# Two attention layers on one core: the first layer's products with the values in two sets, and the queries' piece moved between the key pieces

## The chip, the cores and the metric

The kernel runs on one core of a Trainium2 chip. The metric is the device time of one execution in microseconds. Three executions of the kernel before gave 2612.48 to 2613.71 us, median 2613.1 us.

## What is computed

The batch B is 32, with 112 queries of 320 channels each (20 heads of 16) and a context of 375 tokens of 512 channels, of which the first 77 are "text". Two cross-attention layers follow each other on the same context:

```python
# layer 0: text = ctx[:, :77], ip = ctx[:, 77:] (298 tokens); separate key and value weights for both
q = heads(x @ Wq.T)
out = softmax(q k_text / 4) v_text + softmax(q k_ip / 4) v_ip
x = out @ Wo.T + bo + x
# layer 1: text = the first 371 tokens, ip = the last 4
probs = softmax(q k_text / 4);  text_out = probs v_text
qsem = l2norm(probs text_ctx);  sem = qsem . l2norm(ip_ctx)
probs_ip = softmax(q k_ip / 4 + 0.5 sem) * spatial_mask
x = (text_out + probs_ip v_ip) @ W_out + b_out + x
```

## The kernel before

**One order of stages.** `stage_order` writes down one list of stages for all batches; each engine walks the list and issues its own part of each stage, in that order, with semaphores between the engines. A stage that waits on one engine holds up everything that stands behind it on the same engine. `share` and `in_bank` note for each user of a buffer which signal frees it. PSUM has a three-bank score buffer `ST`, one buffer `PN` of two banks called `PV` and `NS`, and three single banks `R`, handed out in a ring of three to all other products.

**One turn of the loop**, for batch b, has four parts: `groups0(b)`, layer 0 of batch b in five groups of four heads; `groups1(b - 1)`, layer 1 of the batch before; and the row maxima of both layers for what comes next. Among them stand the "pieces" of `ahead(b)`: products for batch n = b + 1 that depend on nothing near. `among0(g)` puts one piece behind the scores of each group of layer 0. Those pieces are, in their order: `keys(n, 0, 0)`, `keys(n, 0, 1)`, `keys(n, None, 0)`, `keys(n, 1, 0)`, then one piece that holds `text_keys(n)` and `queries(n, 0)`, then `keys(n, 1, 1)`; text values follow. `text_keys(n)` makes a third of the text keys of four later batches at once, in the 21 batches in which n is below 28 and no multiple of four. Where n leaves a remainder of three (n = 3, 7, ..., 27) that third holds rows of both layers.

**A group of layer 0** is twelve score matmuls (L690, L693) into `ST`, an exponential on ScalarE (L1126) into one of two buffers `p32`, and 16 matmuls with the values (L707, L710), in which four heads run side by side in strips of 32 columns, each with 17 columns of weights. An f32 matmul has two records, so a group has 32. In `groups0` the product of group g - 1 stands behind the scores and the piece of group g. It is copied by ScalarE to `pvt` (L1024, stage `pv0`), turned by TensorE with an identity (L721, L723, stage `pvT`) and divided and summed by VectorE. `PV_PARTS` says which groups one `pvT` takes: before, groups 0 and 1, then 2 and 3, then 4. The last `pvT` of a batch stands behind the scores of the next layer's first group.

**A key piece** is twelve matmuls (L583 to L587; text keys are eight records of L574 and L575) into a bank R. ScalarE copies the result as bf16 to `kst` (L1024, `kst<-R`), VectorE takes the remainder, a second bf16 part is made by ScalarE for even pieces (`kst<-rem`) and by VectorE for odd ones, and GpSimd makes the third (L1189). Then SyncE writes the three parts to `k_split` in DRAM (L1344; text keys L1340: four DMAs, or eight for the third with rows of both layers, behind which the next text tile `tx` is loaded, L1280). `kst` has two buffers, taken in turn by all key pieces in the order of the list, so the copy of a key piece waits until the writes of the piece two before have landed:

```python
w.wait_ge(k_mm, j + 1)
if j >= 2:
    for signal, value in kw_after[j - 2]:
        w.wait_ge(signal, value)
```

The queries go the same way to `q_split` (L1361, three DMAs). All DMAs are issued by SyncE in the order of the list, among them the `Qs<-ms` writes of the row maxima (L1379), the `xT` load and the reads of keys and queries for the score products (L1354, L1369).

**Layer 1** uses `p32` as well, plus `pr` for rounded probabilities and the two buffers `w2` for weighted ones; `w2` also receives the raw context of a coming batch for a while.

## Time and profile before

| | |
|---|---|
| median of three executions | 2613.1 us |
| the profiled execution's own time | 2613.9 us |
| its span, first to last instruction | 2612.1 us |
| granted TensorE clock, mean | 0.98 |
| TensorE matmuls busy | 2475.8 us (95%) |
| VectorE, ScalarE, GpSimd busy | 63%, 47%, 29% |
| DMA, share of 16 engines | 61.2% |

The busy share of TensorE counts a matmul from its start to its modelled end, and such spans overlap; a matmul takes longer than the distance to the next one. So distances between starts tell more than the busy time. Times in the rows are microseconds from the start of the span.

### The profile page before, as it was taken

What the parts mean: (1) busy time and instruction counts of PE and PEld (TensorE: products, weight loads), DVE (VectorE), ACT (ScalarE), POOL (GpSimd) and SP (SyncE); (2) the same over time, 40 slices, a digit from 0 to 9 for tenths busy, and PEclk for the clock granted to TensorE, in tenths of its full rate; (3) what the DMA queues carried; (4) which work ended last, traced back from release to release, by engine and by line L of the source; (5) the groups of instructions that cost most, each with busy time, mean ns of one, the idle gap of its engine ahead of it and who ended that gap; (6) DMA issues with size and microseconds to landing.
All of it is one profiled execution on the core that took longest, in us unless ns stands there. A gap on an engine that the chain in (4) does not pass through costs nothing.

```text
span 2612.1 us, 64042 instructions
## 1 busy us (share of the span) xinstructions
PE 2475.8 (95%) x26280; PEld 2128.5 (81%) x26280; DVE 1637.9 (63%) x3210; ACT 1232.6 (47%) x2305; POOL 767.3 (29%) x999
## 2 busy tenths in 40 slices
PE   6689999999999999999999999999999999999996
PEld 5578888888888888888888888888888888888874
DVE  2246765666765666776666676566676556677655
ACT  2334445544445544445544445544444544444543
POOL 2123323323323323323322332322322322333222
PEclk7799999999999999999999999999999999999997
DMA  7455777556677555677565777655677655567620
GB/s 181 104 97 87 104 103 93 83 92 92 95 103 91 96 89 86 95 100 107 83 90 86 93 110 101 85 88 86 99 96 104 89 86 89 87 94 101 89 38 7
DMA packets 493225, 241.46 MB, mean 92 GB/s; under 512 B 259627, under 2 KB 492923, under 8 KB 492924
## 3 DMA queue, kind: packets, MB, share of 16 engines
q1 hardware_dynamic: 492934, 237.37, 61.2%
q8 instruction: 208, 3.41, 0.6%
q14 instruction: 83, 0.68, 0.1%
HBM read 171.35 MB, written 64.59 MB: 90 GB/s over the span
## 4 chain that ended last, share of the span: by engine, by line
PE 76%; DVE 17%; issue 2%; SPq 2%; DMA 2%; ACT 1%; POOL 0%; DVEq 0%; ACTq 0%; POOLq 0%
PE ST L690 7%; DVE w L827 6%; PE PN L707 5%; PE R L734 5%; PE R L632 4%; PE R L645 4%; PE R L646 4%; DVE m L911 4%; PE R L583 4%; PE R L584 4%; PE PN L752 3%; PE R L648 3%; PE R L791 3%; PE R L586 3%; DVE w L824 3%; PE ST L672 2%
## 5 line engine op out<-in xcount | busy, mean ns | idle before, releaser
L1126 ACT ACTIVATE p<-ST 128x1344 f32<-128x1344 f32 x320 | 413.6, 1293 | 114.6 <-PE ST L693 110.1
L1256 POOL TENSOR_TENSOR w<-w 128x448 f32<-128x448 f32 (+1 forms) x256 | 330.8, 1292 | 426.3 <-DVE w L824 408.2
L827 DVE SCALAR_TENSOR_TENSOR w<-p,pr 128x1344 f32<-128x1344 f32 x160 | 296.7, 1854 | 174.9 <-ACT pr L1141 161.7
L824 DVE TENSOR_TENSOR rem<-R,kst 128x298 f32<-128x298 f32 (+2 forms) x184 | 91.4, 497 | 455.1 <-ACT kst L1024 455.1
L734 PE MATMUL R<-pr,Gh 128*128 128x448 f32 (+1 forms) x960 | 367.6, 383 | 0.0
L824 DVE TENSOR_TENSOR w<-R,w 128x448 f32<-128x448 f32 (+1 forms) x480 | 281.6, 620 | 71.5 <-PE R L739 61.1
L645 PE MATMUL R<-wvh,ch 128*128 128x320 f32 (+3 forms) x896 | 302.8, 338 | 16.3 <-ACT V0t L1024 12.6
L1189 POOL TENSOR_TENSOR kst<-rem,kst 128x298 bf16<-128x298 f32 (+2 forms) x184 | 151.2, 822 | 483.3 <-ACT kst L1024 262.0
L646 PE MATMUL R<-wvh,cl 128*128 128x320 f32 (+3 forms) x896 | 279.7, 312 | 0.0
L690 PE MATMUL ST<-Qs,Ks 100*128 100x112 bf16 (+1 forms) x3520 | 229.6, 214 | 14.7 <-DMA Qs<-ms 7.6
L690 PEld LDWEIGHTS ST<-Qs,Ks 100*128 100x128 bf16 (+1 forms) x3520 | 184.5, 98 | 67.5 <-issue 35.0
L583 PE MATMUL R<-ch,wkh 128*128 128x298 f32 (+1 forms) x640 | 218.3, 341 | 11.5 <-DVE wkl L824 11.5
L1024 ACT ACTIVATE pvt<-PN 128x112 f32<-128x112 f32 (+1 forms) x320 | 98.1, 306 | 252.7 <-PE PN L756 194.0
L648 PE MATMUL R<-wvl,ch 128*128 128x320 f32 (+3 forms) x672 | 209.7, 312 | 0.0
L1141 ACT ACTIVATE pr<-ST 128x1344 fp32r<-128x1344 f32 x160 | 205.2, 1282 | 0.0
L584 PE MATMUL R<-cl,wkh 128*128 128x298 f32 (+1 forms) x640 | 203.2, 318 | 0.0
L734 PEld LDWEIGHTS R<-pr,Gh 128*128 128x128 f32 (+1 forms) x960 | 176.7, 184 | 22.8 <-issue 6.2
L645 PEld LDWEIGHTS R<-wvh,ch 128*128 128x128 f32 (+3 forms) x896 | 163.3, 182 | 22.0 <-ACT V0t L1024 13.0
L737 PE MATMUL R<-pr,Gl 128*115 128x448 f32 (+1 forms) x480 | 177.1, 369 | 0.0
L739 PE MATMUL R<-pr,Gl 128*128 128x448 f32 (+1 forms) x480 | 176.0, 367 | 0.0
L915 DVE TENSOR_REDUCE m<-ST 112x3 f32<-112x1113 f32 x128 | 168.0, 1312 | 9.0 <-PE ST L674 9.0
L1024 ACT ACTIVATE V<-R 128x320 f32<-128x320 f32 (+2 forms) x160 | 67.6, 437 | 219.0 <-PE R L649 219.0
(185 smaller groups left out, 5834.2 us busy)
## 6 DMA issues: line engine op xcount, KB each, us to landing
Ks<-k_split SPq DMA_DIRECT2D x384, 140.6 KB, 6.1
Ks<-k_split SPq DMA_DIRECT2D x384, 93.8 KB, 8.3
Qs<-q_split SPq DMA_DIRECT2D x384, 70.0 KB, 8.2
w<-in_ctxT SPq DMA_DIRECT2D x31, 750.0 KB, 6.0
k_split<-kst SPq DMA_DIRECT2D x64, 281.2 KB, 3.3
k_split<-kst SPq DMA_DIRECT2D x64, 223.5 KB
q_split<-qst SPq DMA_DIRECT2D x128, 84.0 KB, 2.2
k_split<-kst SPq DMA_DIRECT2D x64, 111.8 KB, 2.5
```

The costliest lines, as they stand in the source:

```text
L583: e.matmul(r[:, 0:t1 - t0], wh[:, k, c0:c0 + 128], h[:, k, t0:t1], start=k == 0, stop=False)
L584: e.matmul(r[:, 0:t1 - t0], wh[:, k, c0:c0 + 128], lo[:, k, t0:t1], start=False, stop=False)
L645: e.matmul(r[0:n, 0:C], h[:, k, :], wh[:, k, :], start=k == 0, stop=False)
L646: e.matmul(r[0:n, 0:C], lo[:, k, :], wh[:, k, :], start=False, stop=False)
L648: e.matmul(r[0:n, 0:C], h[:, k, :], wl[:, k, :], start=False, stop=False)
L690: e.matmul(ST[:, u, S * h:S * h + S], Ks[l][0:m, GH * g + h, 128 * u:128 * u + 128], Qs[l][0:m, GH * g + h, :], start=True, stop=True)
L734: e.matmul(r[0:nj, 0:QW], Gh[0:ROWS[u], q:q + nj], x[0:ROWS[u], QW * u:QW * u + QW], start=u == 0, stop=False)
L824: return e.tensor_tensor(to, x, y, op)
L827: return e.scalar_tensor_tensor(out=to, in0=x, scalar=s, in1=y, op0=op0, op1=op1)
L1126: e.activation(p32[i][:].rearrange("p (u q) -> p u q", u=3), st, ACT.Exp).then_inc(p_whole, 1)
L1141: e.activation(pr[n % 2][:].rearrange("p (u q) -> p u q", u=3), ST[:, :, 0:QW], ACT.Exp).then_inc(p_round, 1)
L1256: e.tensor_tensor(first, first, w2[n % 2][0:ROWS[j], QW * j:QW * j + QW], ALU.add).then_inc(ns_added, 1)
```

## The change

The five products with the values of layer 0 are no longer one behind each group of scores. They come in two sets: groups 0, 1 and 2 in one run behind the scores and the piece of group 3, and groups 3 and 4 in one run behind the piece of the sixth slot. Groups 0, 1, 3 and 4 write two halves of `PV`, group 2 writes `NS`. The probabilities of five groups lie in `p32[0]`, `p32[1]`, `w2[0]`, `w2[1]` and `p32[0]` again. ScalarE copies two groups of `PV` in one instruction, and `NS` in another one. The first two `pvT` stand in the fifth and sixth slot; the parts are groups 0 and 1, then 2, then 3 and 4. The piece with text keys and queries moves from the fifth place to the second, before `keys(n, 0, 1)`. The bookkeeping of who frees what is rewritten to match.

```diff
--- before.py
+++ after.py
@@ -12,7 +12,8 @@
 QW = GH * S
 FV0, FV1 = D + 1, D + 1 + NIP
 ROWS = [128, 128, 115]
-PV_PARTS = [((0, 1), (2, 3), (4,)), ((0, 1, 2, 3), (4,))]
+PV_PARTS = [((0, 1), (2,), (3, 4)), ((0, 1, 2, 3), (4,))]
+PV_SETS = ((0, 1, 2), (3, 4))
 EPS2 = 1e-24
 QPART = [0, 1, 2, 0, 1, 0]
 KPART = [0, 0, 0, 1, 1, 2]
@@ -107,10 +108,10 @@
         todo = ((n, 0, 0), (b, 1, 0), (b, None, 0), (b, 1, 1), (b, None, 1), (b, 1, 2), (b, None, 2), (n, 0, 1), (n, 0, 2))
         tail = values([x for x in todo if x[0] < B])
         if n < B:
-            for l, m in ((0, 0), (0, 1), (None, 0), (1, 0)):
+            yield keys(n, 0, 0)
+            yield text_keys(n), queries(n, 0)
+            for l, m in ((0, 1), (None, 0), (1, 0), (1, 1)):
                 yield keys(n, l, m)
-            yield text_keys(n), queries(n, 0)
-            yield keys(n, 1, 1)
             yield text_values(n)
         yield from tail
 
@@ -142,16 +143,19 @@
         return n
 
     def groups0(b, between):
-        prev = None
+        first = uses[0]
         for g in range(NG + 1):
-            n = scores(b, 0, g) if g < NG else None
+            if g < NG:
+                scores(b, 0, g)
             between(g)
+            if g > 3:
+                turn(b, 0, g - 4)
             if g in (3, 5):
-                turn(b, 0, g // 2 - 1)
-            if g:
-                o.add("pv0", b, g - 1, prev)
-                o.share("PV", 1, ("pv", prev), "pv_read", prev + 1)
-            prev = n
+                which = g // 2 - 1
+                o.add("pv0", b, which, first)
+                o.share("PV", 1, ("pv0", b, which), "pv_read", first + (2, 5)[which])
+                if which == 0:
+                    o.share("NS", 1, ("pv0", b, which), "pv_read", first + 3)
 
     def turn(b, l, part):
         o.add("pvT", b, l, part)
@@ -545,6 +549,14 @@
 
         def rows(name):
             return a[name].rearrange("(k e) c -> e k c", e=128)
+
+        def p0_place(g):
+
+            return (p32[0][:], p32[1][:], w2[0], w2[1], p32[0][:])[g]
+
+        def pv0_place(g):
+
+            return ((PV, 0), (PV, 2 * S), (NS, 0), (PV, 0), (PV, 2 * S))[g]
 
         def v_place(l, t):
 
@@ -693,23 +705,27 @@
                     e.matmul(ST[:, 2, S * GH - S:S * GH], Ks[l][0:m, h, 256:384], Qs[l][0:m, h, :], start=True,
                              stop=True).then_inc(s_mm, 1)
                 elif kind == "pv0":
-                    b, g, n = key
-                    p = p32[n % 2]
+                    b, which, first = key
                     w.wait_ge(v_copied, at("v", b, 0, 2))
-                    w.wait_ge(p_whole, n + 1)
-                    free(w, "PV", ("pv", n))
-                    for u in range(-1, 3):
-                        k = TEXT0 if u < 0 else 119 if u == 2 else 128
-                        for h in range(GH):
-                            hh, q0 = GH * g + h, QW * max(u, 0) + S * h
-                            v, c = (V0t[0:k, hh, :], 0) if u < 0 else (V0[0:k, u, hh, :], S)
-                            if u < 2 or h < GH - 1:
-                                e.matmul(PV[32 * h:32 * h + FV0, c:c + S], v, p[0:k, q0:q0 + S], start=u < 0, stop=u == 2,
-                                         skip_group_check=True)
-                    h = GH - 1
-                    e.matmul(PV[32 * h:32 * h + FV0, S:2 * S], V0[0:119, 2, GH * g + h, :],
-                             p[0:119, 2 * QW + S * h:2 * QW + S * h + S], start=False, stop=True,
-                             skip_group_check=True).then_inc(pv_mm, 1)
+                    for g in PV_SETS[which]:
+                        p, to, c = p0_place(g), *pv0_place(g)
+                        w.wait_ge(p_whole, first + g + 1)
+                        if g in (0, 3):
+                            free(w, "PV", ("pv0", b, which))
+                        elif g == 2:
+                            free(w, "NS", ("pv0", b, which))
+                        for u in range(-1, 3):
+                            k = TEXT0 if u < 0 else 119 if u == 2 else 128
+                            for h in range(GH):
+                                hh, q0 = GH * g + h, QW * max(u, 0) + S * h
+                                v, c0 = (V0t[0:k, hh, :], c) if u < 0 else (V0[0:k, u, hh, :], c + S)
+                                if u < 2 or h < GH - 1:
+                                    e.matmul(to[32 * h:32 * h + FV0, c0:c0 + S], v, p[0:k, q0:q0 + S], start=u < 0,
+                                             stop=u == 2, skip_group_check=True)
+                        h = GH - 1
+                        e.matmul(to[32 * h:32 * h + FV0, c + S:c + 2 * S], V0[0:119, 2, GH * g + h, :],
+                                 p[0:119, 2 * QW + S * h:2 * QW + S * h + S], start=False, stop=True,
+                                 skip_group_check=True).then_inc(pv_mm, 1)
                 elif kind == "pvT":
                     b, l, part = key
                     r = R[slot["R", ("pvT",) + key]]
@@ -940,7 +956,7 @@
                     if i > 1:
                         w.wait_ge(pvT_read, i - 1)
                     if l == 0:
-                        c0 = 128 * part
+                        c0 = GH * D * PV_PARTS[0][part][0]
                         if 3 * b + part:
                             w.wait_ge(o_added, 3 * b + part)
                         if b:
@@ -1116,22 +1132,41 @@
                     copy(ms[0:n, 0, :], r[0:n, 0:S], -1.0).then_inc(m_hi, 1)
                 elif kind == "scores":
                     b, l, g, n = key
-                    i = n % 2
                     st = ST[:, :, 0:QW]
                     w.wait_ge(s_mm, n + 1)
-                    if n >= 2:
-                        w.wait_ge(pv_mm, n - 1)
-                        if l_of[n - 2][0] == 1:
-                            w.wait_ge(w_made, l_of[n - 2][1])
-                    e.activation(p32[i][:].rearrange("p (u q) -> p u q", u=3), st, ACT.Exp).then_inc(p_whole, 1)
-                elif kind in ("pv0", "pv1"):
+                    if l == 0:
+                        to = p0_place(g)
+                        w.wait_ge(pv_mm, n - 3 if g == 4 else n - g)
+                        if b > 1:
+                            w.wait_ge(w_made, NG * (b - 1))
+                        if g in (2, 3):
+                            w.wait_ge(c_low, 4 * min(B, b + 2))
+                            if b > 1:
+                                w.wait_ge(ns_mm, NG * (b - 1))
+                    else:
+                        to = p32[n % 2][:]
+                        w.wait_ge(pv_mm, n - min(g, 1))
+                        if g > 1:
+                            w.wait_ge(w_made, NG * b + g - 1)
+                    e.activation(to.rearrange("p (u q) -> p u q", u=3), st, ACT.Exp).then_inc(p_whole, 1)
+                elif kind == "pv0":
+                    b, which, first = key
+                    if b:
+                        w.wait_ge(pvT, at("pvT", b - 1, 0, 2 * which))
+                    w.wait_ge(pv_mm, first + (2, 5)[which])
+                    copy(pvt[0][:, 3 * which:3 * which + 2, :],
+                         PV[:, 0:4 * S].rearrange("p (g q) -> p g q", g=2)).then_inc(pv_read, 2)
+                    if which == 0:
+                        if b:
+                            w.wait_ge(pvT, at("pvT", b - 1, 0, 1))
+                        w.wait_ge(pv_mm, first + 3)
+                        copy(pvt[0][:, 2, :], NS[:, 0:2 * S]).then_inc(pv_read, 1)
+                elif kind == "pv1":
                     b, g, n = key
-                    l = int(kind == "pv1")
-                    part = [g in groups for groups in PV_PARTS[l]].index(True)
                     w.wait_ge(pv_mm, n + 1)
                     if b:
-                        w.wait_ge(pvT, at("pvT", b - 1, l, part))
-                    copy(pvt[l][:, g, :], PV[:, 0:(2 - l) * S]).then_inc(pv_read, 1)
+                        w.wait_ge(pvT, at("pvT", b - 1, 1, g // 4))
+                    copy(pvt[1][:, g, :], PV[:, 0:S]).then_inc(pv_read, 1)
                 elif kind == "p_round":
                     n, = key
                     k = at("p_round", n)
...
```

## Rows read from the trace of the kernel before

**Rows 1.** Page: busy time by engine; one kind of DMA, median us to landing.

```profile
PE 2475.8 (95%) x26280; PEld 2128.5 (81%) x26280; DVE 1637.9 (63%) x3210; ACT 1232.6 (47%) x2305; POOL 767.3 (29%) x999
...
k_split<-kst SPq DMA_DIRECT2D x64, 281.2 KB, 3.3
```

**Rows 2.** Timeline of TensorE, `groups0` of batch 16: start, duration, line, out<-in, count.

```profile
1332.77 0.72 PE L690 MATMUL ST<-Qs,Ks 102*128 102x112 bf16 x11
...
1335.02 0.30 PE L587 MATMUL R<-ch,wkl 128*128 128x298 f32 x1
1335.16 0.72 PE L690 MATMUL ST<-Qs,Ks 102*128 102x112 bf16 x11
...
1337.36 0.30 PE L587 MATMUL R<-ch,wkl 128*128 128x298 f32 x1
...
1338.48 0.71 PE L690 MATMUL ST<-Qs,Ks 102*128 102x112 bf16 x11
...
1344.82 0.27 PE L723 MATMUL R<-ident_sb,pvt 128*112 128x128 f32 x1
...
1345.91 0.71 PE L690 MATMUL ST<-Qs,Ks 102*128 102x112 bf16 x11
...
1346.52 1.78 PE L574 MATMUL R<-tx,wkt 128*128 128x308 f32 x6
...
1348.65 1.95 PE L632 MATMUL R<-xT,wq 128*128 128x128 f32 x16
...
1353.81 0.49 PE L721 MATMUL R<-ident_sb,pvt 128*112 128x128 f32 x3
...
1355.23 0.71 PE L690 MATMUL ST<-Qs,Ks 100*128 100x112 bf16 x11
```

**Rows 3.** Timeline of TensorE, a product of layer 1 with another behind it.

```profile
1306.07 0.67 PE L752 MATMUL PN<-p,V 128*21 128x112 f32 x19
...
1306.66 0.95 PE L769 MATMUL PN<-w,sel_sb 128*5 128x112 f32 x32
```

**Rows 4.** Timeline of ScalarE, batch 16: the second exponential and the last `pvt` copy.

```profile
1336.67 1.27 ACT L1126 ACTIVATE p<-ST 128x1344 f32<-128x1344 f32 x1
...
1355.37 0.36 ACT L1024 ACTIVATE pvt<-PN 128x224 f32<-128x224 f32 x1 [0.88 <-PE PN L710]
```

**Rows 5.** Timeline of SyncE, batch 16: start of the issue, its length.

```profile
1338.78 2.26 SPq L1379 DMA_DIRECT2D Qs<-ms  x3
...
1351.23 1.97 SPq L1340 DMA_DIRECT2D k_split<-kst  x4
```

**Rows 6.** Timeline of SyncE, batch 14: text keys of both layers.

```profile
1196.83 6.00 SPq L1340 DMA_DIRECT2D k_split<-kst  x8
...
1203.52 1.68 SPq L1361 DMA_DIRECT2D q_split<-qst  x3
```

**Rows 7.** Timeline of SyncE near the start, where text keys stand among others.

```profile
28.41 3.06 SPq L1340 DMA_DIRECT2D k_split<-kst  x4
...
36.92 5.28 SPq L1340 DMA_DIRECT2D k_split<-kst  x8
...
42.89 1.23 SPq L1344 DMA_DIRECT2D k_split<-kst  x2
```

**Rows 8.** Timeline of ScalarE, same stretch; brackets: idle ahead, and its releaser.

```profile
34.61 0.43 ACT L1024 ACTIVATE kst<-R 128x308 bf16<-128x308 f32 x1 [6.78 <-DMA k_split<-kst]
...
44.63 0.48 ACT L1024 ACTIVATE kst<-R 128x371 bf16<-128x371 f32 x1 [6.63 <-DMA k_split<-kst]
45.72 0.51 ACT L1024 ACTIVATE kst<-rem 128x371 bf16<-128x371 f32 x1 [0.61 <-DVE rem L824]
49.81 0.48 ACT L1024 ACTIVATE kst<-R 128x371 bf16<-128x371 f32 x1 [3.58 <-DMA k_split<-kst]
```

**Rows 9.** Windows near the start: span, busy of each engine, granted clock, DMA, GB/s.

```profile
97.00:100.50 3.50, 1.15 (x16) 0.91 (x15) 0.79 (x2) 1.70 (x2) 0.95 (x2) 0.99 0.23 47
100.50:104.00 3.50, 3.50 (x21) 3.34 (x21) 0.00 (x0) 1.70 (x2) 0.00 (x0) 0.51 0.50 147
```

More of the change, by code:

```diff
@@ L1392, in sync @@
             w.wait_ge(d_out[1], 16 * (B // 2))
-        pv_nth, s_nth, l_of, ready_nth, q_before, m_before = {}, {}, {}, {}, {}, {}
-        firsts, rounds, q_last, m_last = 0, 0, None, None
+        pv_nth, s_nth, ready_nth, q_before, m_before = {}, {}, {}, {}, {}
+        q_last, m_last = None, None
         for kind, key in o.stages:
-            if kind in ("pv0", "pv1"):
+            if kind == "pv0":
+                pv_nth[kind, key[0]] = key[2] + NG
+            elif kind == "pv1":
                 pv_nth[kind, key[0]] = key[2] + 1
@@ L1400, in xattn_two_layers @@
                 s_nth[key[0], key[1], key[2]] = key[3] + 1
-                firsts, rounds = firsts + (key[1] == 0), rounds + (key[1] == 1)
-                l_of[key[3]] = (key[1], firsts if key[1] == 0 else rounds)
             elif kind == "k" and key[1] in (1, None):
```

## The prediction, made before the change was run

> **What bounds the kernel now.** I read the page first: TensorE is busy 95% of the span, no other engine over 63% [rows 1]. That share is an average, so I went to the timeline of TensorE over layer 0 of one middle batch, where the whole change lies [rows 2]. From the batch's first scores (1332.77) to the first scores of layer 1 (1355.23) there are 22.46 us, and the starts follow each other without a hole that another engine explains. What is lost there is lost at the seams between kinds of matmul. So the change is worth what it takes from TensorE's queue, less every new wait of that queue. All times below with a plus sign are counted from 1332.77.
>
> **The seams.** Between a key piece and scores with nothing between, the step is 1335.16 - 1335.02 = 0.14 us. With one group's product between them it is 1338.48 - 1337.36 = 1.12 us, so a product on its own costs 0.98 us. Behind a turn it is 1345.91 - 1344.82 = 1.09 us, less a direct step that I don't have from that side (0 to 0.14) [rows 2]. I take 1.0 us for all. What a product costs in the middle of a run is seen in layer 1: 24 records of strips, and then other strip matmuls right behind them, take 1306.66 - 1306.07 = 0.59 us, 0.025 us a record [rows 3]. 32 records make 0.79 us. The change turns five lone products into a run of three and a run of two, so three products go from 1.0 to 0.79 us. With a little for the first key matmul behind a product, that is 0.65 us a batch, and 19.5 us over the 30 middle batches: **-19.5**. (Ends: 0 if the wait ahead of each group breaks the run; -24 if a lone product behind a turn costs the full 1.09.) The number of turned blocks, score matmuls and key matmuls stays the same.
>
> **The last turn of layer 0.** It follows the scores of layer 1 at once and needs the copy of the last product to `pvt`. That copy took 0.36 us for 224 columns and began at 1355.37 [rows 4]; 308 columns took 0.43 [rows 8], so a column costs 0.8 to 0.9 ns and the new copy of 448 columns about 0.55 us. Nothing else is left on TensorE to cover the 0.19 us. In some batches the second part of the key piece delayed the copy before and no longer does. I take **+4.5** for 30 batches (ends 0 and 5.7).
>
> **Cover for the exponentials.** `ST` is a single buffer, so the scores of group g + 1 wait for the exponential of group g. The products that used to stand between are gone from slots 2 and 3. One key piece still covers it: that is the case of slot 1 before, with no stall [rows 2]. But where ScalarE makes the second part of the first key piece ahead of the second exponential, this ends at 1336.67 + 1.27, +5.2, and scores can follow at +5.3 [rows 4]. In the ten batches without text keys only the queries' piece of about 2.1 us stands in slot 2 (it begins at 1348.65 and is over by 1350.75 [rows 2]), and scores would be due at +5.1. Half of those batches: **+1.2** (ends 0 and 3).
>
> **The moved piece, and what it is moved past.** This is the part that I expect to decide. Text keys take a `kst` buffer in the fifth place now and in the second place then. Two key pieces later ScalarE must wait until their writes have landed. Before, that piece stood a whole maxima phase away; then it is `keys(n, None, 0)`, 7 to 9 us later. ScalarE waits in its queue, and behind that copy stand the `pvt` copies, the exponential of group 4 and the copy of `keys(n, 1, 0)`.
>
> When would they land? Text keys start at +3.0 instead of +13.75. The write was issued 1351.23 - 1346.52 = 4.7 us after the text matmuls began [rows 2, 5], so it is ready at +7.7; SyncE is busy with the `Qs<-ms` writes until 1341.04, +8.3 [rows 5]. The kernel's start shows the same pieces close together: text writes issued from 28.41 released ScalarE at 34.61, 6.2 us later, and the eight of the mixed third, issued from 36.92, did so at 44.63, 7.7 us later, after 6.63 us of idle time [rows 7, 8]. So the copy of `keys(n, None, 0)`, wanted at +12.1, would start at +14.5 with four writes and at +16.0 with eight.
>
> With four writes (14 batches) the late copies still come before the turns at +17.1 and +19.6 need them. The chain goes on, though: `keys(n, None, 0)` is written 2.4 us later too, and `keys(n, 1, 1)` waits for its buffer; I estimate that this copy comes about 0.8 us late and delays the last `pvt` copy by 0.5 us in half the batches. **+4** (ends 0 and 14 x 1.2 = 17).
>
> With eight writes (7 batches, six of them with the load of `tx`) SyncE is blocked as well: the eight, the tile and the queries take 1203.52 + 1.68 - 1196.83 = 8.4 us to issue [rows 6], so the writes of `keys(n, 0, 1)` go out at +16.7 instead of +8.3, behind all their data. `keys(n, 1, 0)` needs that `kst` buffer back. The nearest row is the start again: the key writes issued at 42.89, behind eight text writes and a tile, released ScalarE at 49.81, 12.9 us after the first text write [rows 7, 8]; here the queries' three DMAs stand ahead of them too, about 1.5 us more: +8.3 + 14.4 = +22.7. The copy and VectorE's remainder take 45.72 - 44.63 = 1.09 us [rows 8]; then the bank R is free, and the second turn, which is next in the ring for this very bank, can start at +23.9. It is wanted at (1353.81 - 1332.77) - 4.0 + 2.58 = +19.6 (four lone products out, a run of three in) [rows 2]. TensorE stands still for up to 4.3 us. I take 4.0 in six batches and 2.5 in the one without a tile: **+26.5**. If the key writes landed 3.3 us after their issue, the median of such writes on the page [rows 1], the turn could start at +21.2 and the stall were 1.6 us, 11 us in all; the other end is 32.
>
> The page "DMA: Bandwidth & Descriptors" of the Trainium skill (Anatomy of one DMA) gives a DMA a fixed 2.0 us and bytes over 436 GB/s beyond that, an estimate of 2.1 us for one text write of 57.8 KB and 2.5 us for a key write of 223.5 KB. By it the fourth text write lands at +12.0, in time, and `keys(n, 0, 1)` at +19.2 in the mixed batches, which leaves a stall of 0.8 us in seven batches. Rows 7 and 8 speak against it: they show 6.2 us for four small writes, and the measurement decides.
>
> **The clock.** Where TensorE was busy for only 1.15 us of 3.5, the granted clock of the next 3.5 us was 0.51, that is 1.2 GHz instead of 2.4 [rows 9]. A standstill of 3 us or more in each of seven batches may bring the same, at 1.7 us each. I take half of them: **+6** (ends 0 and 12).
>
> **First and last batch.** The last has no pieces, so the exponentials are bare: the run of three delays the scores of group 4, and both last products wait for its exponential, where one of them filled that time before. About 1.6 us. In the first the queries now stand ahead of the first scores and wait for `xT`; that spends its own saving. **+1.6**.
>
> **Sum.** -19.5 + 4.5 + 1.2 + 4 + 26.5 + 6 + 1.6 = +24.3 us. The profiled execution took 2613.9 us (span 2612.1), which gives 2638.2; the median is 0.8 us below that execution, so the forecast is **2637 us**, 0.9% slower.
>
> **Rivals.**
> - *The writes land in time* (faster). The startup rows lie among large loads, and in the middle of a batch the queues are emptier. Then 4, 26.5 and 6 fall away: 2613.9 - 12.2 - 0.8 = 2601 us. With stalls of 0.8 us in seven batches it is 2606.5. The change is faster as long as a mixed batch loses less than 1.7 us (12.2 / 7). For it: each write is small. Against: it is the number of short runs that seems to set those 6.2 us, and that is the same. 15%.
> - *A shorter wait* (no difference): the 3.3 us of the page, a stall of 1.6 us, no clock loss: 2612 us. 10%.
> - *The clock falls each time and for longer*: 2650 us and more. 7%.
> - *The runs save nothing*, because each group waits for its exponential's signal ahead of its first matmul and the array empties there: 2657 us. Against it: in layer 1 a wait stands between the product and what follows, with no gap [rows 3]. 5%.
> - The forecast itself: 63%, with its own range of 2625 to 2648 us.
>
> Slower by over 0.2% (about what a measurement can tell from no change) is 0.63 + 0.07 + 0.05 = 0.75, within it 0.10, faster 0.15. The range reaches from the faster case to the deeper clock loss: 2603 to 2653 us.
>
> **What would show it.** Products in runs of 96 and 64 records with one gap at each end. ScalarE's `kst<-R` waiting for `k_split<-kst` writes in 21 batches, some 2 us with four writes and 4 with eight. TensorE's `R<-ident_sb,pvt` waiting for VectorE's `rem` in seven batches, about 80 x 4 us apart, and low clock behind those stalls. The batches without text keys shorter by about 0.4 us than before. If `kst` never waits, the prediction is wrong and the time is near 2601.

## The result and the profile after

Seven executions of the changed kernel have a median of 2623.8 us (2621.6 to 2630.8), the kernel before beside it 2613.1 (2608.5 to 2618.4): ratio 1.0048, 95% interval 1.0032 to 1.0064. It is slower by 0.5%, inside the range, 13 us below the forecast. Five further executions in a later group of runs gave 2646.0 us (2642.6 to 2652.4) and a ratio of 1.0125 (1.0108 to 1.0142). That the same program is worth two figures is a main finding below.

The profiled execution after took 2628.8 us, 5.0 us above the median; its span is 2626.9 (before 2612.1). TensorE, from the page, against [rows 1]:

```profile
PE 2457.4 (94%) x26280; PEld 2130.8 (81%) x26280; DVE 1632.0 (62%) x3210; ACT 1220.7 (46%) x2241; POOL 768.4 (29%) x999
```

The timeline of TensorE over layer 0 of batch 16 answers to [rows 2]. These are the starts of four of the six groups of scores, the last key record ahead of the first run, the products of the first run and the first of the second, and the last two turns:

```profile
1342.71 0.72 PE L702 MATMUL ST<-Qs,Ks 102*128 102x112 bf16 x11
...
1345.10 0.72 PE L702 MATMUL ST<-Qs,Ks 102*128 102x112 bf16 x11
...
1354.36 0.30 PE L599 MATMUL R<-ch,wkl 128*128 128x298 f32 x1
1354.59 0.39 PE L723 MATMUL PN<-p,V0t 77*17 77x112 f32 x8
...
1355.37 0.37 PE L723 MATMUL PN<-p,V0t 77*17 77x112 f32 x8
...
1356.14 0.37 PE L723 MATMUL PN<-w,V0t 77*17 77x112 f32 x8
...
1357.03 0.72 PE L702 MATMUL ST<-Qs,Ks 102*128 102x112 bf16 x11
...
1362.34 0.27 PE L739 MATMUL R<-ident_sb,pvt 128*112 128x128 f32 x1
1362.54 0.39 PE L723 MATMUL PN<-w,V0t 77*17 77x112 f32 x8
...
1364.21 0.71 PE L702 MATMUL ST<-Qs,Ks 100*128 100x112 bf16 x11
...
1365.11 0.51 PE L737 MATMUL R<-ident_sb,pvt 128*112 128x128 f32 x3
```

The last turn before (behind the scores of layer 1 at 1355.23), and the copy that the last turn after waits for:

```profile
1355.87 0.29 PE L721 MATMUL R<-ident_sb,pvt 128*112 128x128 f32 x1
```

```profile
1364.42 0.54 ACT L1040 ACTIVATE pvt<-PN 128x448 f32<-128x448 f32 x1 [0.71 <-PE PN L726]
```

Layer 0 takes 1364.21 - 1342.71 = 21.50 us instead of 22.46. Inside a run a group costs 0.77 to 0.78 us. From the last key record to the scores behind the run of three it is 2.67 us, which is 2.53 more than a direct step; three lone products cost 2.94. The run of two costs 1364.21 - 1362.34 = 1.87, two lone ones behind turns 2.18. That is the gain: 0.41 + 0.31 = 0.72 us. Layer 0 is shorter by some 0.2 us more because a pair of turned records has left it: the last turn has four records now and had two, and takes 0.38 us instead of 0.16 behind layer 0's scores. The real loss there is that it starts 0.90 us behind the scores of layer 1 instead of 0.64.

The loss is in other places. ScalarE's row in the list of all waits went from 29.5 us, 14 times (five at the start with 19.5 us, nine short ones later), to this, and TensorE's turns got waits of their own:

```profile
ACT kst L1040 <- DMA k_split<-kst: 137.6, 51, 7.1
...
PE R L737 <- DVE rem L840: 11.4, 9, 2.1
PE R L737 <- ACT pvt L1040: 11.0, 12, 2.4
PE R L644 <- DMA xT<-in_xT: 4.8, 1, 4.8
```

Batch 14 is a mixed one (eight text writes, the tile); its first scores start at 1186.76. SyncE, then the copies on ScalarE, then the turns on TensorE, each from the timeline:

```profile
1194.93 5.23 SPq L1375 DMA_DIRECT2D k_split<-kst  x8
1200.21 0.62 SPq L1315 DMA_DIRECT2D tx<-in_txT  x1
1200.87 2.00 SPq L1396 DMA_DIRECT2D q_split<-qst  x3
1202.92 7.99 SPq L1379 DMA_DIRECT2D k_split<-kst  x4
```

```profile
1203.67 0.42 ACT L1040 ACTIVATE kst<-R 128x298 bf16<-128x298 f32 x1 [5.36 <-DMA k_split<-kst]
...
1207.74 0.48 ACT L1040 ACTIVATE kst<-R 128x371 bf16<-128x371 f32 x1 [0.80 <-DMA k_split<-kst]
1209.47 0.48 ACT L1040 ACTIVATE kst<-R 128x371 bf16<-128x371 f32 x1 [1.25 <-DMA k_split<-kst]
```

```profile
1205.65 0.51 PE L737 MATMUL R<-ident_sb,pvt 128*112 128x128 f32 x3 [1.71 <-ACT pvt L1040]
...
1208.86 0.32 PE L737 MATMUL R<-ident_sb,pvt 128*112 128x128 f32 x1 [0.53 <-DVE rem L840]
...
1211.97 0.51 PE L737 MATMUL R<-ident_sb,pvt 128*112 128x128 f32 x3 [0.32 <-ACT pvt L1040]
```

The chain is the forecast one, and its times are near: the copy of `keys(n, None, 0)` starts at +16.9 (forecast +16.0), that of `keys(n, 1, 0)` at +21.0 (+22.7), the second turn at +22.1 (+23.9). What the forecast did not have is that the first turn waits too, for the `pvt` copies behind the first late `kst` copy, so the stall comes in three pieces. Over the seven mixed batches the copy of `keys(n, 1, 0)` starts at +20.1 to +22.2.

**Where the time went.** The distance between the first scores of neighbouring batches, and inside a batch the first scores of layer 1, cut the timeline into comparable pieces. Against the same pieces of before, in us (one profile in each row; "later" is that of experiment 8):

| | mixed batches (7) | other text batches (13) | batches with queries only (10) | up to batch 1 | last batch, end | sum |
|---|---|---|---|---|---|---|
| after | +13.4 | -2.5 | -4.5 | +5.7 | +2.7 | +14.8 |
| after, later | +22.2 | +13.8 | -4.4 | +3.8 | +3.1 | +38.5 |

The ten batches without text keys show the sets undisturbed: 0.91 us less in layer 0, 0.46 more behind it, 0.45 us won, and about 0.5 once the exposed step of five of them (experiment 1) is taken off. That is the same in both profiles. The last batch is longer by the sets too (2.9 us with the sets alone, 0.5 with the move alone). What is left goes with the moved piece.

Two limits of this table: the later profile is 6.4 us above the median of its group, and the profile before has one stretch of half clock, in mixed batch 6 (80.3 us long, the other six 78.1 to 78.6), so the mixed batches really lose 2 us more than the column says.

### The profile page after: what moved, and what is told of

Same layout as the page of the kernel before. It is cut to its first block, busy times and chain, and to the rows that moved or that the text cites. A ratio compares the mean times of both kernels' runs of the same rounds, so it can differ in the third digit from the quotient of the medians.

```text
span 2626.9 us, 63979 instructions
## 1 busy us (share of the span) xinstructions
PE 2457.4 (94%) x26280; PEld 2130.8 (81%) x26280; DVE 1632.0 (62%) x3210; ACT 1220.7 (46%) x2241; POOL 768.4 (29%) x999
## 4 chain that ended last, share of the span: by engine, by line
PE 64%; DVE 18%; SPq 5%; DMA 5%; ACT 3%; issue 3%; POOL 2%; DVEq 0%; ACTq 0%; POOLq 0%
DVE w L843 6%; PE R L750 5%; PE ST L702 5%; PE R L657 4%; PE R L658 4%; DVE m L927 4%; DMA k_split<-kst 4%; PE R L644 4%; PE PN L768 3%; PE R L807 3%; PE R L660 3%; PE PN L723 3%; DVE w L840 3%; PE ST L684 2%; PE R L753 2%
## 5 line engine op out<-in xcount | busy, mean ns | idle before, releaser
L1151 ACT ACTIVATE p<-ST 128x1344 f32<-128x1344 f32 x256 | 331.1, 1293 | 90.6 <-PE ST L705 85.4
L657 PE MATMUL R<-wvh,ch 128*128 128x320 f32 (+3 forms) x896 | 302.4, 338 | 15.3 <-ACT V0t L1040 11.6
L702 PE MATMUL ST<-Qs,Ks 100*128 100x112 bf16 (+1 forms) x3520 | 229.7, 214 | 14.5 <-DMA Qs<-ms 5.2
L750 PEld LDWEIGHTS R<-pr,Gh 128*128 128x128 f32 (+1 forms) x960 | 176.8, 184 | 22.7 <-issue 6.2
L1040 ACT ACTIVATE pvt<-PN 128x112 f32<-128x112 f32 (+2 forms) x256 | 85.5, 343 | 225.8 <-PE PN L772 193.9
L1040 ACT ACTIVATE kst<-R 128x298 bf16<-128x298 f32 (+2 forms) x184 | 81.5, 443 | 197.8 <-DMA k_split<-kst 137.6
```

The source lines that it names most:

```text
L657: e.matmul(r[0:n, 0:C], h[:, k, :], wh[:, k, :], start=k == 0, stop=False)
L702: e.matmul(ST[:, u, S * h:S * h + S], Ks[l][0:m, GH * g + h, 128 * u:128 * u + 128], Qs[l][0:m, GH * g + h, :], start=True, stop=True)
L750: e.matmul(r[0:nj, 0:QW], Gh[0:ROWS[u], q:q + nj], x[0:ROWS[u], QW * u:QW * u + QW], start=u == 0, stop=False)
L1151: e.activation(to.rearrange("p (u q) -> p u q", u=3), st, ACT.Exp).then_inc(p_whole, 1)
```

## The experiments

Eleven kernels in three groups, one chip for each group (experiments 1 to 4; 5, 6, 7 and 9; 8, 10 and 11), each group with its own runs of the kernel before; the ratio is always to those. The changed kernel itself was run again only in the third group. It came out slower there than in its first runs, so experiments 2 to 7 are best compared with the kernel before and with that later run, not with 2624. Figures "by batch" are worked out as in the table above.

**1. The sets alone.** The order of the pieces is the old one:

```diff
-            yield keys(n, 0, 0)
-            yield text_keys(n), queries(n, 0)
-            for l, m in ((0, 1), (None, 0), (1, 0), (1, 1)):
+            for l, m in ((0, 0), (0, 1), (None, 0), (1, 0)):
                 yield keys(n, l, m)
+            yield text_keys(n), queries(n, 0)
+            yield keys(n, 1, 1)
```

> The changed kernel with the pieces in their old order (text keys and queries in the fifth place): the two sets of products alone. Theory A (the sets save seams, the move costs waits): from the trace of the changed kernel, the 23 middle batches without mixed text keys are 0.55 us shorter each, about 16 us over 30 batches, and the last batch 2 to 3 us longer, so 2597 to 2602 us, ratio 0.994 to 0.996, and ScalarE's key copies wait for no write after the start. Theory B (the longer last copy, the thinner cover of the exponentials and the bare last batch eat what the seams give): 2611 us or more, ratio over 0.999.

2613.5 us, ratio 0.9997 (0.9988 to 1.0006): theory A missed. Layer 0 gained 0.46 us a batch instead of 0.96 (the mean of the 23 batches without mixed text keys after the change). ScalarE's key copies do wait for writes after the start, 54 times by up to 2.0 us, but TensorE waits for none of these copies. Timelines of ScalarE and TensorE in batch 16:

```profile
1331.00 0.46 ACT L1040 ACTIVATE kst<-rem 128x298 bf16<-128x298 f32 x1 [0.53 <-DVE rem L840]
1331.36 1.27 ACT L1151 ACTIVATE p<-ST 128x1344 f32<-128x1344 f32 x1
```

```profile
1327.47 0.72 PE L702 MATMUL ST<-Qs,Ks 102*128 102x112 bf16 x11
1329.85 0.72 PE L702 MATMUL ST<-Qs,Ks 102*128 102x112 bf16 x11
1332.69 0.71 PE L702 MATMUL ST<-Qs,Ks 102*128 102x112 bf16 x11 [0.34 <-ACT p L1151]
1335.02 0.72 PE L702 MATMUL ST<-Qs,Ks 102*128 102x112 bf16 x11
```

Scores follow scores at 2.33 to 2.38 us where one key piece of 298 columns stands between, but at 2.84 where ScalarE makes a second part ahead of the exponential. `ST` has one buffer, and with the product gone nothing covers 0.46 us more of ScalarE. In the old order this hits one step in each of the 30 batches, the second or the third by the parity of the piece. So the sets won and lost 0.5 us a batch. That is the prediction's term "cover for the exponentials", which the new order had made small: the moved piece of 4.1 us stands in the exposed place.

**2. The move alone.** The new order in the kernel before.

> The kernel before with the new order of pieces and nothing else. Theory A: the write waits of the text keys and the wait of the first queries for their input come with the move alone: 7 mixed batches at 2 to 4 us and 2 to 3 us at the start, 2630 to 2640 us, ratio 1.006 to 1.010. Theory B: the move costs nothing where products still stand between the groups, because they cover it: 2611 to 2616 us.

2645.9 us (2637.4 to 2650.5), ratio 1.011 (1.0092 to 1.0128). The mixed batches are +23.5 us, the stretch up to batch 1 +6.1, all others together +2.4. So in the mixed batches and at the start the loss belongs to the move and needs no sets. In the 13 text batches with four writes it is different: the move alone costs 0.2 us each (2.3 in all). In experiment 5, which has the sets, the writes released ScalarE equally late (7.1 us after their issue, 7.0 here), and these batches lose 6.0 us where undisturbed sets would win 0.5 each, 6.5. As far as one profile of each shows, the loss in these batches needs both halves of the change. Windows of TensorE at the stall of its first mixed batch (busy times, granted clock behind them):

```profile
268.60:272.00 3.40, 1.89 (x12) 1.58 (x10) 0.76 (x2) 0.56 (x2) 0.27 (x2) 1.00 0.65 135
272.00:278.80 6.80, 5.98 (x57) 5.09 (x58) 2.75 (x8) 2.70 (x5) 2.20 (x4) 0.53 0.39 107
```

Behind the stall the engine runs at half clock (1.2 of 2.4 GHz); four mixed batches here show that.

**3. The text keys two places later**, with the queries moved as before:

```diff
             yield keys(n, 0, 0)
-            yield text_keys(n), queries(n, 0)
-            for l, m in ((0, 1), (None, 0), (1, 0), (1, 1)):
-                yield keys(n, l, m)
+            yield queries(n, 0)
+            yield keys(n, 0, 1)
+            yield keys(n, None, 0)
+            yield keys(n, 1, 0), text_keys(n)
+            yield keys(n, 1, 1)
```

> The changed kernel with the text keys put back behind the fourth key piece, the queries left in the second place. Theory A (it is the text keys' writes and kst): the waits of the key copies go, the queries' early place costs 0.25 us where the second exponential is late and some 2 to 3 us in the first batch: 2601 to 2606 us, ratio 0.995 to 0.998. Theory C (it is the queries' early place: the late input, the order of the DMAs): no better than the changed kernel, 2620 us or more.

2628.7 us, ratio 1.0047 (1.0034 to 1.0061): theory A missed. The number is theory C's, its cause is not: the mixed batches lose nothing any more (-1.6 us for the seven), but the other text batches lose 11.6 us, 8.0 of them in batches 5 and 13, where half clock follows the stall. The wait has only moved; in the mixed batches it is 2.3 to 3.9 us. SyncE, ScalarE and TensorE in batch 13:

```profile
1128.13 0.38 SPq L1381 DMA_DIRECT2D k_split<-kst  x1
```

```profile
1133.41 0.48 ACT L1042 ACTIVATE kst<-R 128x371 bf16<-128x371 f32 x1 [5.71 <-DMA k_split<-kst]
```

```profile
1135.59 0.51 PE L739 MATMUL R<-ident_sb,pvt 128*112 128x128 f32 x3 [3.29 <-ACT pvt L1042]
```

Now two `kst` users stand in one slot, and `keys(n, 1, 1)` waits for the write of `keys(n, 1, 0)`, issued only 5.3 us before. So another place that puts three of these pieces close together waits too.

**4. No wait for the text writes.** The text DMAs of later tiles read the constant `kip` instead of `kst`, in the same shapes, and the copy two pieces later doesn't wait for them. This kernel writes other numbers into the text keys; whether its writes are as fast as those from `kst` was not tested.

```diff
-                kw_after.setdefault(j, []).append((d_kw[l_][j % 2], kw_count[l_, j % 2]))
+                kw_after.setdefault(j, [])
+                if key[1] != "t" or not key[0]:
+                    kw_after[j].append((d_kw[l_][j % 2], kw_count[l_, j % 2]))
...
+                                t_from = kip[r0:r1, 0, :, 0:TEXT0] if b else kst[j % 2][r0:r1, :, TEXT0 * i:TEXT0 * i + TEXT0]
```

> The changed kernel, but the DMAs of text keys after the first tile read a constant tensor of the same size instead of kst (so the text keys in k_split are other numbers), and no key copy waits for them. The same DMAs are issued in the same places. It parts the two waits in the mixed batches. If the wait for the text writes themselves holds TensorE: the 7 mixed batches lose most of their 19 us, 2605 to 2610 us. If it is the next key write, issued behind eight text writes, a tile and the queries: the fourth key copy still starts about 21 us after the batch's first scores, the second turn still waits, and only the first turn's wait (up to 1.7 us) moves into it: 2617 to 2624 us.

2640.8 us, ratio 1.0097 (1.0083 to 1.0111), outside both ranges. By batch it splits cleanly. The 13 text batches gain 6.5 us, 0.50 each, which is what undisturbed batches gain: what the text keys cost there is this wait. The mixed batches lose 30.9 us, where the move alone on the same chip lost 23.5. TensorE and the windows around the stall of batch 2 (first scores at 250.32):

```profile
273.45 0.46 PE L739 MATMUL R<-ident_sb,pvt 128*112 128x128 f32 x1 [3.45 <-DVE rem L842]
```

```profile
269.40:272.80 3.40, 0.60 (x4) 0.29 (x2) 0.00 (x0) 0.46 (x1) 0.00 (x0) 1.00 0.72 163
272.80:279.60 6.80, 6.14 (x84) 5.27 (x85) 3.63 (x10) 2.53 (x5) 2.31 (x4) 0.50 0.38 105
```

The first turn no longer waits (+17.0 in all seven), but the second starts at +23.1 (median of the seven), no earlier than with the wait (+22.1 in the first profile, +23.4 in the later one). So the wait for the text writes themselves doesn't set the end there; the write of `keys(n, 0, 1)`, queued behind them, does. TensorE runs up to it and stands there in one piece, 2.6 to 5.5 us, and half clock follows in six of the seven batches; it was four with the move alone and four in the later profile of the changed kernel.

**5. The tile later.** The load of `tx` is moved from behind the eight text writes to behind the text values.

> The changed kernel, with the load of the next text tile moved from behind the eight text writes to behind the text values, in the six batches that have it. Theory: in a mixed batch TensorE waits for the third key piece but one, whose copy waits for a key write that is queued behind eight text writes, the tile and the queries. The tile's issue takes 0.7 us and its data lie ahead as well, so that write should land 0.7 to 1.5 us earlier and the seven stalls of 19 us in all should shrink by 4 to 9 us: 2615 to 2620 us. Rival: it is the small text writes alone that hold the queues; then the tile is worth nothing and the time stays at 2624.

2643.7 us, ratio 1.0107 (1.0089 to 1.0125). The mixed batches lose 20.7 us; experiments 7 and 8, which have the tile in its place, lose 23.0 and 22.2. So the tile is worth about 2 us, by one profile of each; the forecast of 4 to 9 was wrong. The level of the time is that of the unaltered kernel in experiment 8.

**6. The move left out in the mixed batches** and in the first turn.

```diff
+            early = n > 1 and n % QUAD != 3
             yield keys(n, 0, 0)
-            yield text_keys(n), queries(n, 0)
-            for l, m in ((0, 1), (None, 0), (1, 0), (1, 1)):
+            if early:
+                yield text_keys(n), queries(n, 0)
+            for l, m in ((0, 1), (None, 0), (1, 0)):
                 yield keys(n, l, m)
+            if not early:
+                yield text_keys(n), queries(n, 0)
+            yield keys(n, 1, 1)
```

> The changed kernel, with the text keys and queries moved only in batches whose third of the text keys has four writes, or none; in the seven mixed batches and in the first turn they stay in their old fifth place. Theory: the move costs nothing where it has four writes or fewer, and the sets then gain 0.5 us a batch. The mixed batches fall to about zero against the kernel before (sets alone there: minus 0.4 in layer 0, plus 0.4 behind it), so 19 us come back, and 2 to 3 us of the first turn: 2600 to 2605 us. Rival: the stall in the mixed batches stands for something that moves with the bytes of the writes, and appears elsewhere in the same batch; then 2612 or more.

2626.6 us, ratio 1.0037 (1.0024 to 1.005). The forecast of 2600 to 2605 missed. What it said of the mixed batches holds: they come out at 0.0 us against before, and experiments 5 and 7 in the same group are 17 to 18 us slower. But the 13 other text batches lose 16.1 us here, where the first profile of the changed kernel had won 2.5 with the same instructions. My assumption that four writes cost nothing had rested on one profile.

**7. Two copies for groups 3 and 4**, group 4 in `NS`, so that the first copy can run beside the second product.

```diff
-                    copy(pvt[0][:, 3 * which:3 * which + 2, :],
-                         PV[:, 0:4 * S].rearrange("p (g q) -> p g q", g=2)).then_inc(pv_read, 2)
...
+                    else:
+                        copy(pvt[0][:, 3, :], PV[:, 0:2 * S]).then_inc(pv_read, 1)
+                        w.wait_ge(pv_mm, first + 5)
+                        copy(pvt[0][:, 4, :], NS[:, 0:2 * S]).then_inc(pv_read, 1)
```

> The changed kernel, with groups 3 and 4 copied to pvt by two instructions, group 3 while the product of group 4 still runs (group 4 goes to the other PSUM bank for this). Theory: the 0.4 us that each batch is longer behind layer 0's scores is the last turn waiting for the 448-column copy of 0.54 us; a copy of 224 columns takes 0.36 us, so 0.18 us a batch come back, 5.5 us: 2618 us. Rival: the 0.4 us are the additional turned blocks at a place of their own, or something in layer 1; then 2624.

2644.7 us, ratio 1.0118 (1.01 to 1.0135). In total it looks like a failure, yet the batches without text keys took 55.86 us behind layer 0 instead of 56.12 (medians; before it was 55.76), a gain of 0.26. That is the whole of what the last turn waits longer (0.90 against 0.64 us). The rival is true beside it: a pair of turned records (0.22 us) now stands there that stood in layer 0, which costs nothing in sum. The total is high by the same loss in text and mixed batches as in its neighbours.

**8. The changed kernel again**, unaltered, in the third group.

> The changed kernel once more, unaltered. In the previous group of runs text batches with the same pieces in the same order took 1 to 2 us more than in the first profile of the changed kernel: the same DMAs, issued at the same places, landed later (the third of four text writes at +14.1 to +14.3 instead of +12.8). Theory: where the pieces are moved, the time hangs on how soon small writes land, and that differs between chips; beside the kernel before on the same chip the changed one is slower by 0.4% where they land early and by 1% (2640 us) where they land late, and nothing between is excluded. Rival: the growth came from the edits themselves; then 2624 here, 0.4 to 0.5% slower, whatever the landings.

2646.0 us against 2614.4 before, ratio 1.0125 (1.0108 to 1.0142). This is the control. Batch 16, first scores at 1354.51: SyncE and ScalarE.

```profile
1362.83 2.08 SPq L1375 DMA_DIRECT2D k_split<-kst  x4
```

```profile
1369.89 0.42 ACT L1040 ACTIVATE kst<-R 128x298 bf16<-128x298 f32 x1 [3.14 <-DMA k_split<-kst]
...
1376.02 0.48 ACT L1040 ACTIVATE kst<-R 128x371 bf16<-128x371 f32 x1 [2.34 <-DMA k_split<-kst]
```

The same batch in the first profile after:

```profile
1351.02 2.08 SPq L1375 DMA_DIRECT2D k_split<-kst  x4
```

```profile
1357.15 0.42 ACT L1040 ACTIVATE kst<-R 128x298 bf16<-128x298 f32 x1 [2.20 <-DMA k_split<-kst]
...
1363.23 0.48 ACT L1040 ACTIVATE kst<-R 128x371 bf16<-128x371 f32 x1 [1.70 <-DMA k_split<-kst]
```

Both issue the four writes at +8.3, in 2.08 us. They release ScalarE 6.1 us after the first issue in the first profile and 7.1 us in this one. Over the 13 batches with four writes the median is 6.2 us in the first and 7.3 here; in experiments 2, 5, 6 and 7, on the other two chips, it is 7.0, 7.1, 7.5 and 7.4. So the first profile is the one that stands apart, and the edits of those experiments are not what made the writes late. With that microsecond TensorE's turns wait for `pvt` copies 20.9 us in all instead of 11.0, and for `rem` 13.7 instead of 11.4. In mixed batch 10 the first turn waits for

```profile
900.93 0.86 PE L737 MATMUL R<-ident_sb,pvt 128*112 128x128 f32 x3 [3.08 <-DVE rem L840]
```

where it was 2.13 us, and the windows show what follows:

```profile
896.40:899.80 3.40, 1.45 (x9) 1.14 (x7) 0.00 (x0) 0.00 (x0) 0.00 (x0) 1.00 0.85 103
899.80:906.60 6.80, 5.67 (x30) 5.24 (x34) 2.44 (x7) 3.77 (x7) 1.97 (x4) 0.50 0.59 138
```

Six such stretches lie in the middle of this profile, none in the first; at half clock for 23.8 us in all, they cost at most 12 us (an estimate from those lengths). Four are in mixed batches, two in text batches, 1 and 21. That of batch 21 stands at

```profile
1773.70 0.86 PE L737 MATMUL R<-ident_sb,pvt 128*112 128x128 f32 x3 [1.84 <-ACT pvt L1040]
```

**9. The second parts on VectorE.** Sets with the old order; the two layer-0 pieces never use ScalarE for their second part.

```diff
+        def by_vector(key):
+            return nk[key] % 2 == 1 or (key[0] and key[1] == 0)
...
-                    if j % 2 == 0:
+                    if not by_vector(key):
                         w.wait_ge(k_rem, j + 1)
```

> Sets alone (the old order of the pieces), and the second bf16 part of the two layer-0 key pieces made by VectorE always, instead of by ScalarE where the piece is even. Theory: sets alone gained nothing because, without a product between, scores follow scores at 2.33 us, which ScalarE just meets with an exponential of 1.29 us and one copy; where it has to make a second part of 0.46 us as well, the exponential and with it the next scores come 0.5 us late, once in each batch. Then 30 x 0.5 = 15 us come back: 2598 us, with distances of 2.3 to 2.4 us in the second and third step of each batch. Rival: it is the wait for a kst buffer that delays ScalarE; then the 2.84 stays and the time is 2613.

2599.7 us (2597.0 to 2605.5), ratio 0.9941 (0.9927 to 0.9954). TensorE in batch 16:

```profile
1322.73 0.72 PE L705 MATMUL ST<-Qs,Ks 102*128 102x112 bf16 x11
...
1325.07 0.72 PE L705 MATMUL ST<-Qs,Ks 102*128 102x112 bf16 x11
...
1327.40 0.72 PE L705 MATMUL ST<-Qs,Ks 102*128 102x112 bf16 x11
```

The steps are 2.33 us here and in all 30 middle batches (2.37 to 2.39 for the first step), and ScalarE still waits for `k_split` writes 96.5 us in all, 70 times. So the exponential behind the second part was the cause in experiment 1, not the wait for `kst`.

**10 and 11. With two copies, and with lone products in the last batch.**

> Sets with the old order of the pieces and the layer-0 second parts on VectorE (the previous 2600), plus groups 3 and 4 copied to pvt by two instructions from two PSUM banks. Theory: the last turn of each batch then waits for a copy of 0.36 us instead of 0.54, and the stretch behind layer 0's scores falls from 56.12 by 0.2 to 0.25 us (55.87 in batches without text keys when two copies were tried with the moved pieces): 6 to 7 us in all, 2593 us. Rival: VectorE with its new work or the wait for kst is late for other reasons and takes the gain; 2600.

> The same with two copies, and in the last batch each group's product alone behind the next scores, as before. Theory: the last batch has no pieces, so the sets leave its exponentials bare; its layer 0 took 15.5 us with sets and 12.45 before, and 3 us come back: 2590 us, 0.9% below the kernel before. Rival: the last batch ends on something else; then the same as with two copies.

2592.2 us, ratio 0.9915 (0.99 to 0.9929), and 2588.4 us (2586.2 to 2592.1), ratio 0.990 (0.9885 to 0.9914). The first scores of layer 1 and the last turn behind them with two copies:

```profile
1340.51 0.71 PE L704 MATMUL ST<-Qs,Ks 100*128 100x112 bf16 x11
...
1341.15 0.51 PE L739 MATMUL R<-ident_sb,pvt 128*112 128x128 f32 x3
```

The turn follows after 0.64 us, not after 0.90. Lone products in the last batch bring its layer 0 from 15.1 back to 11.9 us. The step from 2592.2 to 2588.4 us is small beside the ranges of the executions (2589.4 to 2595.0 and 2586.2 to 2592.1), which overlap. The last kernel is 58 us faster than the changed one in the same group, with the same sets of products in the middle batches: it differs in the order of the pieces and in these three edits.

## Why the prediction was right, step by step

| step | forecast | first profile | later profile |
|---|---|---|---|
| seams | -19.5 | about -23 | about -23 |
| last turn | +4.5 | +7.8 | +7.8 |
| cover of the exponentials | +1.2 | +0.8 | +0.8 |
| four-write batches | +4 | +4.1 | +20 with the clock |
| mixed batches | +26.5 | +17 | +26 with the clock |
| clock | +6 | 0 | at most 12, in the two rows above |
| first and last batch | +1.6 | +8.4 | +6.9 |

- **Seams and last turn.** Together -15 was forecast; 30 batches at about -0.5 are -15. The 7.8 is 30 x 0.26 (experiments 7 and 10), above the upper end of 5.7 that I gave from the length of the copies alone; the seams are then the rest, about -23, and the gaps of batch 16 give 30 x 0.72 = 21.6 directly. Experiments 1 and 9 show that the gain is real where the exponentials are covered.
- **Cover.** 0.17 us in five batches: the step over the queries is 2.84 there and 2.67 in the other five. Right, but I did not see that the move was what kept it small; for that I should have costed each half of the change alone.
- **Four writes.** The copy of `keys(n, None, 0)` was forecast for +14.5 and began at +14.4 (1357.15 - 1342.71), in the later profile at +15.4. The chain behind it, to the last `pvt` copy, was named with 0 to 17 us; the first profile lies at 4. The later one lies at 20, beyond the end, with two stretches of half clock in it. This is the term that the later runs show as too small.
- **The page's rule.** "DMA: Bandwidth & Descriptors" of the Trainium skill (Anatomy of one DMA), 2.0 us fixed and the bytes beyond, put the fourth write at +12.0. That section speaks of DMAs issued by GpSimd, one at a time; these are issued by SyncE, several in a row. The fourth write released the copy at +14.4 and +15.4, and `keys(n, 0, 1)` in mixed batch 14 released its at +21.0, not +19.2. Rows of this kernel's own start were the better guide.
- **Mixed batches.** In the first profile the size was off by a third: the writes released `keys(n, 1, 0)` 0.5 to 2.6 us earlier than the start's rows had said, and the stall is split over two or three turns. Experiments 2 and 6 show that the loss is the move's, experiment 4 that the key write behind the text writes ends it. The tile, which I had counted into the queue, adds little (experiment 5).
- **Clock.** Forecast as a coin toss for the seven mixed batches; none of them in the first profile, four in the later one, and two stretches in text batches, which the forecast didn't have.
- **Ends.** Too small. In the last batch 2.7 to 3.1 us instead of 1.6 for both; in the first turn the queries wait 4.8 us for `xT`, which I had set against their own saving. The start also differs between executions: experiments 1, 9, 10 and 11, all with the old order there, reach batch 1 between 3.4 us earlier and 2.2 us later than before. So its share can't be cut finer.

Of the signs named, the waits of ScalarE, the waits of the turns and the shorter batches without text keys (0.45 us) are there in the first profile, the low clock only in the later one. The rivals: the writes don't land in time; the shorter wait would have released the copy of `keys(n, 1, 0)` at +20.0, and the median of the seven is +21.0; the runs do save. The deeper clock loss (2650 us) is close to the later runs in its number but not in its mechanism: the clock fell in four of the seven mixed batches, and the text batches with four writes bring the rest.

The mechanism was right, the total in part by luck. In the first profile mixed batches and clock were forecast 15 us too high together, the ends 7 us too low. In the later one mixed batches with their clock are below the forecast too (26 against 26.5 + 6), and 16 us more in the four-write batches outweigh it. The forecast of 2637 lies between the two measurements, 2624 and 2646, because these errors change places.

What stays open: why the small writes landed a microsecond earlier in the first profile than on the three chips afterwards, whether by the chip or by something that differs from occasion to occasion; and why the sets make the four-write batches sensitive to it, where the move alone did not. The program and the issue times are the same; the chip of the first runs isn't known, and no run here tells more. My expectation for experiment 8 laid it to the chip; that is not shown.

## What to carry to other kernels

When a producer with few buffers is moved, count the distance to the user two places on in time, not in pieces, and count what its queue still holds. A product that looks like a loss at two seams may be the cover of another engine's exponential; before removing it, see what that engine does ahead of the exponential, and give that work to an engine that is free at that moment (here VectorE, though it is busier on average). Where the end hangs on when a DMA lands, measure on more than one occasion before believing a few tenths of a per cent.

## What the runs showed of the hardware

- The same four writes of 57.8 KB, issued at the same place, released their reader after 6.1 us on one occasion and 7.1 us on another. The kernel before hardly moved (2613.1, 2614.0, 2616.4 and 2614.4 us on the four occasions), the changed one by 22 us.
- Stalls of up to 2.4 us, split over several turns, left TensorE's granted clock at 1.00 between batch 1 and the last batch in the first profile after. Stalls of 3.08 and 3.45 us were followed by 0.50 (the windows above), but so was one of 1.84 us in text batch 21 of the later profile, whose turn then took 0.86 us instead of 0.51. The length of the last stall alone doesn't decide it. The kernel before has a stretch too, in batch 6, with no idle time of TensorE above 0.61 us ahead of it:

```profile
612.50:615.90 3.40, 2.09 (x12) 1.25 (x11) 3.33 (x10) 1.24 (x6) 0.00 (x0) 1.00 1.39 130
615.90:619.30 3.40, 3.40 (x15) 3.15 (x14) 2.06 (x4) 0.41 (x1) 0.00 (x0) 0.50 1.13 228
```

- A copy from PSUM by ScalarE took 0.36 us for 224 columns and 0.54 us for 448, and the turn that waits for it started 0.26 us later with the longer one (0.90 against 0.64 us behind the scores).
